# Four blocks in one launch: the local layers' output projection placed ahead of the turning of weights, which is cut into row halves, and Block 1's second queries and keys placed ahead of the first exponentials

## What is computed

```
x = layernorm(x + attention16(x))     # Block 1: 16 heads of 16, keys and queries over 512 tokens
x = layernorm(x + slots_experts(x))   # Block 2
x = layernorm(x + retention(x))       # Block 3
x = layernorm(x + local2(x))          # Block 4: two layers of the following
    h = shift_token(x)                # the second half of the channels comes from the token before
    q, k, v = split(h @ wqkv)         # 8 heads of 64
    q, k = rotary(l2norm(q) * qs), rotary(l2norm(k) * ks)
    sim = 8 * q @ k.T over this window of 128 tokens and the one before, key j from i - 128 to i
    x = x + (softmax(sim) @ v) @ wo
    h = layernorm(shift_token(x))
    a, g = split(h @ w1 + b1);  x = x + (a * gelu(g)) @ w2 + b2
```

## Time and profile before

| | us |
|---|---|
| median of three runs | 2335.92 |
| the profiled execution, its own device time | 2333.25 |
| its span in the trace | 2331.40 |
| PE busy in the span | 2239.6 |
| DVE busy | 1635.1 |
| ACT busy | 1254.6 |
| POOL busy | 732.4 |

### The profile page before, as it was taken

How to read it: one execution, slowest core, us unless ns; L and a number is a source line. 1 busy time by engine, 2 the same in 40 slices (tenths; PEclk the granted TensorE clock), 3 DMA queues, 4 the chain that set the end, 5 groups by cost and what they waited for, 6 DMA issues and landing times.

```text
span 2331.4 us, 42446 instructions
## 1 busy us (share of the span) xinstructions
PE 2239.6 (96%) x16257; PEld 1316.2 (56%) x16306; DVE 1635.1 (70%) x4252; ACT 1254.6 (54%) x2823; POOL 732.4 (31%) x730
## 2 busy tenths in 40 slices
PE   7999999999998999989899999999999999999998
PEld 3333333334634867756566666666666666666665
DVE  6788888886502746668777677677767777787763
ACT  4666666665222622247666656665665665566640
POOL 3344323321111411144433233333333333333321
PEclk7999999999998999999999999999999999999999
DMA  7454343333397020010000000000001000000001
GB/s 240 151 158 121 117 119 122 112 91 109 157 422 297 2 91 19 28 39 3 5 6 6 5 2 6 6 2 32 15 6 53 6 15 24 19 6 24 22 23 40
DMA packets 68617, 158.44 MB, mean 68 GB/s; under 512 B 6256, under 2 KB 49120, under 8 KB 63936
## 3 DMA queue, kind: packets, MB, share of 16 engines
q1 hardware_dynamic: 65856, 146.55, 17.8%
q0 software_dynamic: 2560, 9.18, 1.7%
HBM read 116.39 MB, written 35.13 MB: 65 GB/s over the span
## 4 chain that ended last, share of the span: by engine, by line
PE 73%; DVE 14%; DMA 4%; ACT 4%; issue 3%; POOL 1%; SPq 0%; another core or an unknown queue 0%; POOLq 0%; DVEq 0%; ACTq 0%
PE banks L2073 10%; PE banks L2051 7%; PE banks L1932 6%; PE banks L1946 5%; PE banks L232 4%; PE banks L274 4%; PE banks L2033 3%; PE banks L245 3%; PE banks L1976 3%; PE banks L1991 3%; DMA arena<-in_e_W 3%; DVE arena L483 2%; PE banks L1455 2%; PE banks L1958 2%; PE banks L300 2%
## 5 line engine op out<-in xcount | busy, mean ns | idle before, releaser
L483 DVE TENSOR_REDUCE arena<-banks 128x1 f32<-128x512 f32 x512 | 322.6, 681 | 61.2 <-PE banks L232 60.4
L395 ACT ACTIVATE arena<-banks 128x512 f32<-128x512 f32 x512 | 280.3, 596 | 136.1 <-PE banks L245 112.4
L2073 PE MATMUL banks<-arena 128*128 128x512 f32 x640 | 293.2, 594 | 1.0 <-DVE arena L2258 1.0
L2155 ACT ACTIVATE arena<-arena 128x256 f32<-128x256 f32 (+1 forms) x512 | 286.5, 562 | 5.0 <-DVE arena L2264 4.5
L2411 POOL TENSOR_TENSOR arena<-arena 128x512 f32<-128x512 f32 x128 | 162.8, 1272 | 379.8 <-DVE arena L2295 379.8
L1932 PE MATMUL banks<-arena 128*128 128x512 f32 x512 | 241.5, 594 | 2.8 <-DVE arena L2295 2.8
L232 PE MATMUL banks<-arena 96*128 96x512 bf16 x512 | 202.9, 400 | 14.6 <-DVE arena L483 8.9
L2407 POOL TENSOR_TENSOR arena<-arena 128x16 f32<-128x16 f32 x64 | 189.4, 2959 | 5.4
L2127 ACT ACTIVATE arena<-arena 128x256 f32<-128x256 f32 (+1 forms) x256 | 102.1, 471 | 162.9 <-DVE arena L2240 162.9
L2073 PEld LDWEIGHTS banks<-arena 128*128 128x128 f32 x640 | 115.5, 190 | 126.7 <-issue 116.5
L245 PE MATMUL banks<-arena 128*128 128x512 bf16 x463 | 174.6, 382 | 3.1 <-ACT arena L395 2.2
(11 more groups left out here) (304 smaller groups left out, 4225.7 us busy)
## 6 DMA issues: line engine op xcount, KB each, us to landing
arena<-in_e_W SPq DMA_DIRECT2D x16, 2048.0 KB, 15.6
arena<-stacks SPq DMA_DIRECT2D x64, 384.0 KB, 4.7
arena<-in_e_Wg SPq DMA_DIRECT2D x8, 2048.0 KB, 17.6
stacks<-arena SPq DMA_DIRECT2D x32, 384.0 KB, 2.5
stacks<-arena SPq DMA_DIRECT2D x32, 256.0 KB, 2.8
arena<-dens POOLq DMA_DIRECT2D x32, 256.0 KB, 4.8
arena<-in_xT SPq DMA_DIRECT2D x8, 512.0 KB, 7.8
stacks<-arena SPq DMA_DIRECT2D x32, 128.0 KB, 2.6
```

Source lines behind the costliest of these rows:

```text
L395: e.activation(ex[:, j], self.psum[:, self.exp_bank1(k)], ACT.Exp).then_inc(s["a_e"], 1)
L483: e.tensor_reduce(split(self.maxima[n % 2][:, 0:16], TILES, UNIT)[:, t, j:j + 1], self.psum[:, k % 3], AX.X, ALU.max, negate=True).then_in ...
L2073: i = e.matmul(bank, weights[:, c], self.hT[:, c], start=c == 0, stop=c == 1)
L2155: k = e.activation(pr[:, h, at:], pr[:, h, at:], ACT.Exp, bias=mx[:, h:h + 1], scale=rn[:, h:h + 1], accum_out=den[:, h:h + 1])
```

## The change

Ten things, of which the first nine are in Block 4:

1. PE: the output projection of tile d stands ahead of all turning of weights of tile c.
2. PE: the turning takes heads in couples of pairs, in row halves: 12 transpositions of 64 rows (64 columns moving) for a couple, 24 for a tile, in place of 16 of 128 rows (8 and 16 for a first tile, which had 8). Only the parts inside the window are turned, so a pair's bank holds 384 columns in place of 512.
3. DVE copies the lower halves of both couples (2 x 384 columns, 2 x 256 for a first tile) in a row ahead of the first rotation; ACT copies the upper halves, both ahead of the second set of exponentials.
4. The division writes from one raw buffer to a second one in the order that the turning wants, in place of in place.
5. Values: four matmuls of 256 columns in place of two of 512; those of odd heads take their tokens from a copy with its halves swapped.
6. POOL makes that copy (`gpsimd4_swap`, four copies of 128 x 64) ahead of each tile's own work.
7. The attend of a first tile uses quadrants too (16 matmuls in place of 8 of twice the area); all tiles then sum two banks, so ACT has a copy and DVE a sum for first tiles too.
8. The turned weights have two buffers, so their copies wait for the attend one tile earlier.
9. In slot 2, ACT's turn for Block 3's last sequence stands behind the mlp part.
10. Block 1: the four tasks of queries and keys of the second sequence move from steps (0, 0), (0, 1), (2, 0), (2, 1) to (-1, 0) to (-1, 3).

```
@@ tasks1
-                    at[4 * k + 2 * h, side].append(("qk", 2 * k + 2 + h, side))
+                    at[(4 * k + 2 * h, side) if k else (-1, 2 * h + side)].append(("qk", 2 * k + 2 + h, side))
@@ tensor4
             self.tensor4_mlp(e, w, n, 2)
+            if d is not None:
+                self.tensor4_out(e, w, d)
             if c is not None:
                 self.tensor4_weights(e, w, c, 0)
                 self.tensor4_weights(e, w, c, 1)
-            if d is not None:
-                self.tensor4_out(e, w, d)
-            if c is not None:
-                self.tensor4_weights(e, w, c, 2)
-                self.tensor4_weights(e, w, c, 3)
             self.tensor4_mlp(e, w, n, 3)
@@ tensor4_values
+        w.wait_ge("t_swap", i + 1)
+        out = split(self.psum[:, 2], PAIRS, 2, HD4)
+        for hh in range(2):
+            for c in range(CHUNKS):
+                at = 1 - c + t * P
+                tokens = self.swapped[i % 2][:, c] if hh else self.xT[:, b, c, at:at + P]
+                k = e.matmul(out[:, :, hh], tokens, split(self.wqkv4[:, c, 2], PAIRS, 2, HD4)[:, :, hh], start=c == 0, stop=c == 1, skip_group_check=True)
@@ tensor4_weights
+    def tensor4_weights(self, e, w, i, couple):
+        banks = [self.bank4("w", i, 2 * couple + half) for half in range(2)]
+        w.wait_ge("t_pn", 2 * i + couple + 1)
+        w.wait_ge("t_pna", 2 * i + couple + 1)
+        self.emptied4(w, "w", i, 2 * couple)
+        self.emptied4(w, "w", i, 2 * couple + 1)
+        places = [(0, 0, 1), (1, 1, 2), (2, 2, 3)] if i % TILES else [(3, 1, 0), (2, 2, 1)]
+        for n in range(2):
+            for place in places:
...
+                    rows, at = slice(64 * half, 64 * half + 64), 512 * (2 * couple + n) + P * source
+                    k = e.transpose(banks[half][:, 192 * n + 64 * to:192 * n + 64 * to + 64], self.probs[1][rows, at:at + P], self.ident[rows, rows])
@@ scalar4
             self.scalar4_mlp(e, w, n, 2)
             if c is not None:
+                self.scalar4_weights(e, w, c, 0)
                 self.scalar4_weights(e, w, c, 1)
             if b is not None:
                 self.scalar4_exp(e, w, b, 1)
-            if c is not None:
-                self.scalar4_weights(e, w, c, 3)
@@ vector4
             if c is not None:
                 self.vector4_weights(e, w, c, 0)
+                self.vector4_weights(e, w, c, 1)
             if a is not None:
                 self.vector4_rotate(e, w, a, 0)
...
-            if c is not None:
-                self.vector4_weights(e, w, c, 2)
             if a is not None:
                 self.vector4_rotate(e, w, a, 1)
@@ gpsimd4
             if n < TILES4:
+                self.gpsimd4_swap(e, w, n)
                 self.gpsimd4_tile(e, w, n)
```

166 lines of the change are left out of this document (90 added, 76 removed).

## The result

The changed kernel takes 2367.27 us, median of four runs (2365.83 to 2367.88), against 2335.70 for the kernel before, now of four runs. The ratio is 1.0135, with a 95% interval of 1.0118 to 1.0152. That is 32 us slower; forecast were 12 slower, with a range that reached to 2371. The profiled execution's span is 2365.3 us, 33.9 more than before. A second series of the same kernel, on another chip, gave 2364.74 and 1.0129 (1.0112 to 1.0145).

What follows compares the result with a forecast made beforehand. The prediction took PE's work as the bound, with DVE slackless in one steady slot of four. Block 1 -2, early slots +8, steady part +5, ends +1 gave +12: 2345 us profiled, 2348 median, range 2323 to 2371.

Steps and rivals of the forecast that it cites:

- Block 1: Moved query and key tasks: later first exponentials against four tasks gone from PE, -2 us, bounds -6 and +4.
- a cycle of the steady part: Four successive slots of Block 4's steady part: +0.4 us together, fourteen times, +5 us, bounds -1 and +26.
- DVE's chain of type 0: The one slot in four where DVE has no slack: its first copy starts 1.48 us later, the scores 1.1 later.
- a wait of 1.5 or more: Sign at the second half of the scores: such a wait for DVE once per cycle, about 12 us in eight cycles.
- The other slots of a cycle: Steady part: two full slots gain 0.45 us each, DVE's slack covering the later copy; the first-tile slot loses 0.18.
- the sum of 1.29: Full slot, from the projection's end to mlp part 3: switch, transpositions, DVE's copy and wait take 1.29 us, against 1.74.
- Layer 2's first-tile slot: Steady part, slot with a first tile, layers not told apart: 1.05 us in place of 0.87, a loss of 0.18.
- Early slots: Six slots of Block 4 without mlp pieces in part 2, hanging on DVE: some 1.35 us each, +8, bounds +4 and +11.
- The part I gave to POOL's copies: Early slots of Block 4: POOL's swap runs beside DVE's L2303 and stretches it, 0.5 us more.
- Load-bound: Rival on the turning: each row half is held 0.124 us, a couple takes 0.74, total 2371 us; chance 0.18.
- The chain gives way: Rival: DVE's lateness at the scores is taken up, all three full slots gain 0.45 us, total 2323; chance 0.18.
- cancelling: Rival for the whole kernel: early slots +4, Block 1 -5, steady part 0, total 2335 us; chance 0.22.

Runs made afterwards that it cites:

- the order alone: The kernel before with only PE's output projection moved ahead of all four groups of turned weights, which stay full transpositions: 2361.18 us, ratio 1.0111.
- the kernel with the output between: Changed kernel with Block 1's table as before and the output projection back between the two couples, DVE's and ACT's copies in old order: 2323.91 us, again 2325.92.

## Why the prediction was wrong in size

The direction was as forecast, and so was the mechanism in Block 4: DVE's later copy, felt at the scores and in the early slots. The sum had +12 and the medians show +32. Three steps failed. The clock behind the new waits of the early slots was put at nothing, and it costs 4.4 us. Block 1 was counted as a gain of 2, with four tasks gone from PE, where a longer wait took the fourth one's time back; it is a loss of 3 to 5 (7.6 in the profiled execution). And a cycle of the steady part was put at +0.4 and is +0.72, in layer 2 +1.19, so +12 in place of +5. Term by term:

- **DVE's chain of type 0.** Forecast: the scores 1.1 late. Measured: their second half comes 9.25 us behind the slot's start in place of 7.80, of which 0.31 had been won in the slot before, so 1.14 late. Forecast for the waits for L2351's successor was about 12 us in the eight cycles, measured 10.4. Right, and the order alone shows the same wait. One sign was missed: a wait of 1.5 or more was named, and it is 1.31, since PE gains only 0.31 ahead of it and starts the first half of the scores later as well.
- **The other slots of a cycle.** Forecast -0.45, -0.45, +0.18, measured -0.31, -0.31, +0.26. From the start of projection or turning to part 3 it was 3.48 us before and is 3.06 now, so 0.42 is gained, and the sum of 1.29 for switch, transpositions, copy and wait was right to 0.05. The wait in it is 0.27 and not about half a microsecond. But from there to the next slot it takes 3.54 (1935.42 to 1938.96) in place of 3.43: the first record, 0.1 longer, stands behind row halves now and behind the full array before, and I had not priced this way back. With 0.03 for the values it makes up the 0.34 a cycle, 4 of the 7 us that the steady part was off.
- **Layer 2's first-tile slot.** Forecast +0.18, measured +0.74. I took "type 1 and 2 have slack" from layer 1. In layer 2, DVE has the final statistics and normalisation in this slot, 4 us more, and starts 1.3 later; its first maxima then hold the bank of part 2's piece. 0.47 a cycle, 2.4 us in five cycles. The row of DVE's waits that I leaned on the earlier trace rows is a sum over both layers and hides this.
- **Early slots.** Forecast +8, measured +12.5. With three of the four falls gone they are +8.1, so the chain was sized about right and the step that failed was to leave the clock out. The prediction noted in Block 1 that the clock falls and rises, and priced it there; it then put new waits of 2 us into PE's timeline in Block 4 without asking the same question. The part I gave to POOL's copies was wrong too, by another sum that happened to fit: no L2314 of slots 3 to 7 was stretched by them (each takes 0.69 us); they were stretched themselves. In its place stands PE's wait of 0.78 us for ACT's copy of the values, ahead of each projection, which the forecast had as a part of 1.1.
- **Block 1.** Forecast -2, measured +2.7 by medians (+7.6 in the profiled execution, at slot 0's start). The first exponential came at 57.27 against my 55.8, so 8.0 later than before and not 6.5. The two tasks gone from unit 0 gave 5.8 back, which leaves 2.2; my own terms, 6.5 less 5.0, give 1.5 and not the 0.5 of the sum, a slip of 1 us. Unit 2's two gave 3.2, so just in front of 91 us the changed table is ahead by 1.1. There the step failed that counted four tasks as gone: the fourth stood beside three table loads of ACT, PE waits there anyway, and its time came back as 1.95 of longer wait, with 1.5 for the clock behind it, 2.3 behind in all. The other 5 us of the profiled execution are the late transfer, which strikes either table.
- **Slot 0.** Forecast nothing, measured +1.5 in both traces of the changed kernel, none in the kernel with the output between at its first run and 1.4 at its second. The kernel before with nothing moved but Block 1's four tasks has it too (23.1 in place of 21.7), so it is not Block 4's change. A fall of the clock again, see below.
- **The rivals.** "Load-bound" gave 2371, near the measured time, and is false: 24 transpositions start within 0.75 us, and the time went elsewhere. By the Trainium skill, TensorE: Matmul & The Clock Gate, section LDWEIGHTS, a load of 128 columns takes 0.107 us (an estimate from its columns over 1.2 per ns), so the twelve of each row half 1.3; the trace disagrees, with one every 0.06 us. A time that fits is no evidence for its mechanism. "The chain gives way" did not occur, nor did cancelling.

## What to carry to other kernels

Before moving work out of a place, look what waits there anyway: a task beside a wait can be free, and it may cover a bank's release or a table load that shows in no row of waits until the task is gone. When a change creates a wait of 2 us on TensorE, price the clock behind it as well as the wait. And where a chain of one engine is the limit, look for its own idle gap first: one copy moved into VectorE's wait for POOL brought 10 us, nearly as much as halving the transpositions.

The version that came of it, with the row halves, the output projection between the couples, VectorE's second copy behind the rotations and Block 1 as before, takes 2315.48 us, 0.9921 of the kernel before.

## What the hardware showed that was not expected

The granted clock does not follow from the length of a wait alone. Of the changed kernel's waits for the rotation in slots 3 to 7, 1.85 to 2.00 us each, one was not followed by a fall, that at the start of slot 5, though it is as long as the longest:

```profile
1091.22 1.98 PE L1926 MATMUL banks<-arena 128*128 128x512 f32 x4 [2.00 <-DVE arena L2306]
```

In slot 0 PE waits 2.70 us for the same DVE operation before and after. Before, the transpositions behind it take 0.91 us, after 1.62:

```profile
1014.09 0.91 PE L1517 MATMUL banks<-arena 128*128 128x128 f32 x6 [2.70 <-DVE arena L1687]
```

```profile
1021.68 1.62 PE L1517 MATMUL banks<-arena 128*128 128x128 f32 x6 [2.70 <-DVE arena L1687]
```

and the windows behind them, of before and of after, grant 1.00 and 0.57:

```profile
1014.00:1018.00 4.00, 3.91 (x50) 1.00 0.00 0
```

```profile
1021.00:1025.00 4.00, 3.32 (x39) 0.57 0.00 0
```

PE's work for ten microseconds ahead is the same in both. The kernel with the output between shows both outcomes at this place, in its two traced executions. So a wait of 2 to 3 us put the clock at risk here, and what decided whether it fell was not settled.
